# Squared norms of K and Q moved from the attention loop into the QKV stage, and a per-head bound prepared half a head early

## What is computed

```
x = x + layernorm(attn(layernorm(x)))
x = x + layernorm(ffn(layernorm(x)))
attn: qkv = h @ Wqkv.T + b; softmax(q k.T / sqrt(128)) v; @ out_w.T + out_b
ffn:  fake_quant(x) @ fake_quant(kernel) + fake_quant(bias); relu; fake_quant
```

## Time and profile before

| quantity | us |
|---|---|
| timed, median of 2 runs | 7679.78 (7638.61 and 7720.94) |
| the profiled execution, its own time | 7434.41 |
| its span on the slowest core, from the first to the last instruction | 7432.8 |
| spans of the 8 cores | 7412.6 to 7432.8 |

### The profile page before, as it was taken

One profiled execution on the slowest core, in us unless ns is written; L12 is line 12 of the kernel. 1 busy time (PEld: TensorE's weight loads), 2 busy tenths in 40 slices (PEclk: granted clock), 3 DMA queues, 4 the chain that ended last, 5 costly groups with the idle time before them and its releaser, 6 DMA issues.

```text
span 7432.8 us, 43416 instructions; the slowest of 8 cores (7412.6 to 7432.8 us)
## 1 busy us (share of the span) xinstructions
PE 4127.7 (56%) x16028; PEld 1555.4 (21%) x16028; DVE 2157.3 (29%) x2411; ACT 1295.3 (17%) x1457; POOL 93.5 (1%) x106
## 2 busy tenths in 40 slices
PE   0049999987666666667766666664443413030303
PEld 0024444432222222222222222221111101010101
DVE  4512221111111111111111111121221255757566
ACT  1300000003333333333333333320000000000001
POOL 0000000000000000000000000000000000000000
PEclk9999999998888888888888888876666656565656
DMA  6553221111000000000000000029999940000010
GB/s 167 192 127 71 60 68 44 44 49 34 23 23 23 23 23 23 23 23 23 1 23 23 23 23 23 3 50 162 154 157 168 156 80 28 31 31 31 25 40 23
DMA packets 372388, 431.24 MB, mean 58 GB/s; under 512 B 178931, under 2 KB 334579, under 8 KB 355283
## 3 DMA queue, kind: packets, MB, share of 16 engines
q0 software_dynamic: 137344, 159.40, 15.1%
q1 hardware_dynamic: 193638, 168.10, 8.0%
q10 hardware_dynamic: 41200, 100.96, 3.8%
HBM read 461.70 MB, written 100.94 MB: 76 GB/s over the span
## 4 chain that ended last, share of the span: by engine, by line
PE 43%; DVE 20%; ACT 15%; DMA 13%; issue 4%; DVEq 3%; SPq 2%; ACTq 0%; POOLq 0%
PE psB L442 9%; DMA wob<-wo 9%; PE psA L838 8%; PE psA L847 7%; ACT PT L863 6%; PE psB L509 6%; ACT PT L865 6%; PE psA L1093 3%; PE psC L790 2%; PE psA L1360 2%; PE psD L798 2%; SPq L366 1%; SPq L1336 1%; DVE nkt L694 1%; PE psB L1033 1%
## 5 line engine op out<-in xcount | busy, mean ns | idle before, releaser
L442 PE MATMUL psB<-h1fm,wfc 128*128 128x512 bf16 x3072 | 665.8, 380 | 471.4 <-DMA h1fm<-h1h 471.4
L863 ACT ACTIVATE PT<-psA 128x1024 bf16<-128x1024 f32 x512 | 524.4, 1024 | 1596.6 <-PE psA L847 1596.6
L838 PE MATMUL psA<-negCB,onesm 128*128 128x512 bf16 x2048 | 580.2, 409 | 350.8 <-ACT PT L865 279.3
L885 DVE CAST ctxst<-psC 128x512 bf16<-128x512 f32 x64 | 44.3, 691 | 2440.9 <-PE psD L798 2440.9
L1353 PE MATMUL psA<-bqB,onesm 128*128 128x512 bf16 x64 | 27.6, 431 | 1090.7 <-DMA xqfm<-xqh 749.4
L847 PE MATMUL psA<-Qh,Kh 128*128 128x512 bf16 x2048 | 624.5, 435 | 0.0
L790 PE MATMUL psC<-PT,Vh 128*128 128x512 bf16 x2048 | 578.7, 409 | 26.7 <-ACT PT L865 26.7
L798 PE MATMUL psD<-PT,ones_bf 128*1 128x512 bf16 x2048 | 525.0, 378 | 0.0
L865 ACT ACTIVATE PT<-psA 128x1024 bf16<-128x1024 f32 x512 | 521.8, 1019 | 0.0
L442 PEld LDWEIGHTS psB<-h1fm,wfc 128*128 128x128 bf16 x3072 | 301.1, 98 | 835.6 <-issue 474.9
L509 PE MATMUL psB<-wvb,h1fm 128*128 128x512 bf16 x2048 | 468.9, 382 | 0.0
(11 more groups left out here) (175 smaller groups left out, 3156.2 us busy)
## 6 DMA issues: line engine op xcount, KB each, us to landing
wob<-wo POOLq DMA_DIRECT2D x64, 2048.0 KB, 20.7
xst<-x SPq DMA_DIRECT2D x32, 1024.0 KB, 5.3
ktst<-kernT SPq DMA_DIRECT2D x16, 1024.0 KB, 6.7
wfc<-wqk POOLq DMA_DIRECT2D x32, 512.0 KB, 7.8
h1h<-h1t ACTq DMA_DIRECT2D x32, 512.0 KB, 2.8
khh<-kout ACTq DMA_DIRECT2D x16, 1024.0 KB, 8.5
vhh<-vst ACTq DMA_DIRECT2D x128, 128.0 KB, 1.7
Kh<-khh SPq DMA_DIRECT2D x16, 1024.0 KB, 7.1
```

The costliest lines, as they stand in the source:

```text
L442: ins = nc.tensor.matmul(psB[g % 2][:], wfc[fc % 2][:, dc * 128:(dc + 1) * 128], h1fm[:, dc * 4096 + tt * 512: dc * 4096 + (tt + 1) * 512] ...
L838: nc.tensor.matmul(pa[:, off:off + 512], onesm[:], negCB[:], start=True, stop=False, skip_group_check=True)
L863: nc.scalar.activation(PT[sp][:, 0:1024], psA[0][:], AF.Exp, scale=SMS)
```

## The change

1. In stage 2, behind the last group of each Q or K head, the squared norms are now made from `qout` or `kout`, piece by piece of 512 tokens: VectorE squares a piece into `nsq2` (one buffer), TensorE sums it into one of four rows of `psA`, VectorE takes the maximum (K) or copies the row to `nrow2` (Q). Q rows go to DRAM (`nqh`), the 16 maxima of K too (`mkh`).
2. In stage 3 the chain at the head of each head is gone. `emit_cchain` does the rest of it (load of the row, logarithm, halving plus K term, exponential, scaling) for head h+1 behind the second block (`qt == 1`) of head h, and for head 0 at the start of the stage. `negCrow` has two buffers.
3. To make room, `kst` has one buffer instead of two; its load for head h waits until head h-1 is quantised.

```
+        for tt in range(ntt):
+                v.drain()
+                v.tensor_mul(nsq2[:], obuf[par][:, tt * 512:(tt + 1) * 512],
+                             obuf[par][:, tt * 512:(tt + 1) * 512]
+                             ).then_inc(c_sq3.h, 1)
+            wt("tensor", c_sq3, c_sq3.n)
+                nc.tensor.matmul(pa[0:1, off:off + 512], ones_bf[:, 0:1],
+                                 nsq2[:], start=True, stop=True
+                                 ).then_inc(c_nm.h, 1)
+            wt("vector", c_nm, c_nm.n)
+                v.drain()
+                if is_q:
+                    v.tensor_copy(nrow2[0:1, tt * 512:(tt + 1) * 512],
+                                  pa[0:1, off:off + 512]).then_inc(c_nr.h, 1)
+                else:
+                    v.reduce_max(nkt[0:1, tt:tt + 1], pa[0:1, off:off + 512],
+                                 axis=AX).then_inc(c_nr.h, 1)
...
+    def emit_cchain(hh):
+        if hh >= 1:
+            wt("sync", c_negC, hh)
+            nc.sync.dma_start(nq_sb[0:1, :], nqh[hh:hh + 1, :]
+                              ).then_inc(d_nq[hh % 2].h, 16)
+        wt("scalar", d_nq[hh % 2], d_nq[hh % 2].n)
+            nc.scalar.activation(kqa[0:1, :], nq_sb[0:1, :], AF.Ln)
+            v.tensor_scalar(kqt[0:1, :], kqa[0:1, :], 0.5,
+                            lnmk[0:1, hh:hh + 1], OP.mult, OP.add)
+            nc.scalar.activation(kqa[0:1, :], kqt[0:1, :], AF.Exp)
+            nc.vector.tensor_scalar(negCrow[par2][0:1, :], kqa[0:1, :],
+                                    -1.001 / 128.0, -1.0 / 128.0,
+                                    OP.mult, OP.add).then_inc(c_negC.h, 1)
...
-        if h >= 2:
-            wt("sync", f_kn[par], h // 2)
+        if h >= 1:
+            wt("sync", f_kn[0], h)
...
+        wt("tensor", d_k3[par], 16 * (h // 2 + 1))
+        wt("tensor", d_q3[par], 16 * (h // 2 + 1))
...
             emit_pvden(qt, 7)
+            if qt == 1 and h + 1 < H:
+                emit_cchain(h + 1)
```

More of the change, by code:

```diff
@@ L56, in build_program @@
     denh = nc.dram_tensor("denh", [64, 512], F32, kind="Internal").ap()
+    nqh = nc.dram_tensor("nqh", [16, 2048], BF16, kind="Internal").ap()
+    mkh = nc.dram_tensor("mkh", [1, 16], F32, kind="Internal").ap()
     sksh = nc.dram_tensor("sksh", [2048], F32, kind="Internal").ap()
@@ L114, in build_program @@
     c_sq3 = sem("c_sq3")
+    d_nq = [sem("d_nq0"), sem("d_nq1")]
+    s_nq = sem("s_nq")
     c_nm = sem("c_nm")
@@ new lines, in build_program, with _ @@
+        if is_q:
+            @on("vector")
+            def _():
+                v = nc.vector
+                v.drain()
+                v.tensor_scalar_max(nrow2[0:1, :], nrow2[0:1, :], 1e-6
+                                    ).then_inc(c_nr.h, 1)
+            c_nr.inc(1)
+            wt("scalar", c_nr, c_nr.n)
+            if head >= 2:
+                wt("scalar", s_nq, s_nq.n - 16)
+            @on("scalar")
+            def _(head=head):
+                nc.scalar.dma_start(nqh[head:head + 1, :], nrow2[0:1, :]
+                                    ).then_inc(s_nq.h, 16)
+            s_nq.inc(16)
+        else:
+            @on("vector")
+            def _(head=head):
+                v = nc.vector
+                v.drain()
+                v.reduce_max(sm1[0:1, head:head + 1], nkt[0:1, 0:8], axis=AX
+                             ).then_inc(c_nr.h, 1)
+            c_nr.inc(1)
@@ L470, in build_program, with _ @@
+    @on("vector")
+    def _():
+        v = nc.vector
+        v.drain()
+        v.tensor_scalar_max(sm1[0:1, 0:16], sm1[0:1, 0:16], 1e-12
+                            ).then_inc(c_nr.h, 1)
+    c_nr.inc(1)
+    wt("scalar", c_nr, c_nr.n)
+    @on("scalar")
+    def _():
+        nc.scalar.dma_start(mkh[0:1, :], sm1[0:1, 0:16]).then_inc(s_nq.h, 16)
+    s_nq.inc(16)
     wt("tensor", c_bias, 1)
@@ L601, in build_program, with _ @@
         p3be.inc(1)
+    wt("sync", s_nq, s_nq.n)
+    @on("sync")
+    def _():
+        nc.sync.dma_start(nkt[0:1, :], mkh[0:1, :]).then_inc(d_mk.h, 16)
+    d_mk.inc(16)
+    wt("scalar", d_mk, d_mk.n)
+    @on("scalar")
+    def _():
+        nc.scalar.activation(lnmk[0:1, :], nkt[0:1, :], AF.Ln
+                             ).then_inc(p1s.h, 1)
+    p1s.inc(1)
+    wt("vector", p1s, p1s.n)
+    @on("vector")
+    def _():
+        nc.vector.drain()
+        nc.vector.tensor_scalar_mul(lnmk[0:1, :], lnmk[0:1, :], 0.5
+                                    ).then_inc(c_nr.h, 1)
+    c_nr.inc(1)
+    def emit_cchain(hh):
+        par2 = hh % 2
+        if hh >= 1:
+            wt("sync", c_negC, hh)
+        wt("sync", c_nr, 1)
+        @on("sync")
+        def _(hh=hh):
+            nc.sync.dma_start(nq_sb[0:1, :], nqh[hh:hh + 1, :]
+                              ).then_inc(d_nq[hh % 2].h, 16)
+        d_nq[hh % 2].inc(16)
+        wt("scalar", d_nq[hh % 2], d_nq[hh % 2].n)
+        @on("scalar")
+        def _():
+            nc.scalar.activation(kqa[0:1, :], nq_sb[0:1, :], AF.Ln
+                                 ).then_inc(p1s.h, 1)
+        p1s.inc(1)
+        wt("vector", p1s, p1s.n)
+        @on("vector")
+        def _(hh=hh):
+            v = nc.vector
+            v.drain()
+            v.tensor_scalar(kqt[0:1, :], kqa[0:1, :], 0.5,
+                            lnmk[0:1, hh:hh + 1], OP.mult, OP.add
+                            ).then_inc(c_sq3.h, 1)
+        c_sq3.inc(1)
+        wt("scalar", c_sq3, c_sq3.n)
+        @on("scalar")
+        def _():
+            nc.scalar.activation(kqa[0:1, :], kqt[0:1, :], AF.Exp
+                                 ).then_inc(p1s.h, 1)
+        p1s.inc(1)
+        wt("vector", p1s, p1s.n)
+        @on("vector")
+        def _(par2=par2):
+            nc.vector.drain()
+            nc.vector.tensor_scalar(negCrow[par2][0:1, :], kqa[0:1, :],
+                                    -1.001 / 128.0, -1.0 / 128.0,
+                                    OP.mult, OP.add).then_inc(c_negC.h, 1)
+        c_negC.inc(1)
+    emit_cchain(0)
     smm_rel = {}
@@ L644, in build_program @@
[L644 to L743, removed]
@@ L904, in build_program @@
         s_ctx[par].inc(16)
-        wt("vector", d_kn[par], 16 * (h // 2 + 1))
+        wt("vector", d_kn[0], 16 * (h + 1))
         wt("vector", p3be, p3be.n)
@@ L911, in _ @@
             v = nc.vector
-            v.tensor_mul(kqt[:], kst[par][:], RSKb[:])
+            v.tensor_mul(kqt[:], kst[0][:], RSKb[:])
             v.drain()
```

92 lines of the change are left out of this document (39 added, 53 removed).

## The result

The changed kernel takes 7713.73 us at the median of 12 executions (7496.69 to 7851.44), the kernel before 7541.08 us at the median of 10 (7432.84 to 7720.94). The ratio is 1.0105, with a 95% interval of 1.0059 to 1.0151: slower, by about 1%.

The account below looks back on a forecast made before the run. TensorE was taken to bound stage 2, working without a break, with about 1060 us idle in attention. Terms -430 - 22 + 66 + 408 + 68 = +90 gave 7524 us profiled, 7773 timed; 8 in 10 range 7630 to 7870.

Parts of the forecast that it names:

- The first of its cases: Whole kernel: the summed forecast, +93 us on the timed scale, 7773 us, own range 7700 to 7845; chance 0.58.
- the step to the timed scale: Whole kernel: timed median taken as 3.3% above the profiled execution, so +90 became +93 us and 7773 us timed.
- Chain removed between heads: Attention, between heads: first bound matmul of a new head starts 28.7 us earlier, 15 times, -430 us.
- Head 0: Start of attention: L816 starts at 1689.9 instead of 1712.27, -22 us.
- Chain inserted: Attention, behind the second block: the chain delays the third block by 4.4 us, 15 times, +66 us.
- Squares and sums: Stage 2, behind each Q or K head: TensorE waits through steps of 2.16 us each, +408 us.
- The clock after each gap: Stage 2: the first group behind each gap starts at a low clock, 32 losses of 2.1 us, +68 us.
- Attention otherwise: Rest of attention: the head restarts as it did, nothing taken; up to +45 us as the upper bound.
- Stages behind attention: After attention: the sum held no term for these stages.
- The fourth case: Stage 2: excess of timed runs lies in unbroken stretches, gaps give back 137 us; -47, timed 7631; chance 0.13.
- The rival of slow hand-overs: Stage 2's 160 steps: 0.46 us both ways, a step of 2.67, +172 us, timed 7857; chance 0.20.
- That of a clock that stays up: Stage 2's gaps: steps of 1.87 us and no cold start, -24 us, timed 7655; chance 0.09.

Follow-up runs that it names:

- experiment 7: Changed kernel with stage 2's steps in the next head's stream, chain spread over the second block, quantisation behind the next head's first cast: 6894.43 us.
- experiment 4: Changed kernel with the bound's chain taken apart and spread behind the exponentials of steps 2 and 4 of the second block: 7435.41 us.
- experiment 1: Changed kernel without the 192 squares, small sums and maxima of stage 2, their rows filled with a constant: 7032.33 us.
- experiment 3: Changed kernel with each of the 192 steps of stage 2 made twice: 7907.8 us.
- experiment 8: Changed kernel with two buffers for the squares in stage 2, the next square made ahead of the maximum: 7356.76 us, 0.9919 to the kernel before.
- experiment 9: Kernel before with two unread VectorE products of 2.29 us each ahead of the second block's evacuation: span of 7502.8 us on core 1, 81 more than before.
- the fillers: Changed kernel with six large matmuls into an unused accumulator ahead of each small sum of stage 2: 7402.36 us.

## Why the prediction came out as it did

The forecast was slower by 1.2%, and 1.05% was measured. The first of its cases, with the largest chance, took place; what it gave as within 2% is, by the interval, a slow-down of 0.6 to 1.5% and not no change. My sum pointed that way, and only the bound of 2% made it "the same". Two steps failed all the same: the step to the timed scale, and in the sum the term for attention. Term by term, on core 1 or as a mean where it says so:

- *Chain removed between heads:* -28.7 us each; the gap fell from 44.27 to 15.85, -28.4. Right, also in what is late next; experiment 7 removed that, and nothing stood behind it.
- *Head 0:* -22; -25 from the end of V to the first L853.
- *Chain inserted:* +4.4 each; 3.22 to 7.39, that is +4.2 over all 16 heads, since the last has none: 4.45 where it stands. Right, and experiment 4 took it back.
- *Squares and sums:* +408; gaps of 8.36 and 17.08 us less 0.22 each, 16 of each, are 400. A step is 2.06 us and not 2.16, for the most part because a third of the small matmuls (62 of 192) still ran at 2.4 GHz; I had given that to one or two per gap. The experiments 1, 3 and 8 confirm its working.
- *The clock after each gap:* +68; the first group takes 5.40 instead of 3.45, 62 us.
- *Attention otherwise:* "I take nothing". This step failed: -22 us, the largest miss of the sum. I had held that "the head restarts as it did". But the low stretches moved: a block had 6.4 us at 1.2 GHz before, and the four have 8.0, 5.5, 8.3 and 3.8 now. Experiment 9 shows that a longer gap alone moves them. The time at 1.2 GHz is nearly the same in sum (25.8 and 25.6 us a head), and the gain did not come in experiment 9, so where it comes from stays open.
- *Stages behind attention:* nothing; +18 on core 1 and 7 as a mean of four cores, also open.
- The sum was +90 for a profiled execution; measured are +64 between the shortest executions and +73 on core 1.

The step to the timed scale failed as well, and the range stood on it. "The timed median is 3.3% above the profiled execution; scaled by it": the 3.3% came from two executions. Over ten, the median of the kernel before is 1.5% above its shortest, 7432.84 us. The changed kernel's shortest, 7496.69, lies under the 7630 that was my lower end, while the sum before the scaling, 7524, is 27 us from it. That the median of 7713.73 is near 7773 is luck, as its distance from the shortest, 2.9%, is no term of the sum.

What the excess consists of stands in the profile after. The first window is of core 5, the second of core 6 of the same die, both in the V part (columns as above):

```profile
1912.00:2030.00 118.00, 115.58 (x441) 47.64 (x438) 18.31 (x27) 0.00 (x0) 0.53 (x1) 0.81 0.09 29
```

```profile
1880.00:1990.00 110.00, 109.42 (x500) 49.79 (x509) 20.74 (x30) 0.00 (x0) 0.00 (x0) 1.00 0.11 36
```

Core 5 has a granted clock of 0.81, and a matmul in its stream takes 0.27 us instead of 0.22. So there is a third level; the prediction's "no run here shows a third level" was true of the trace before and is not true of this one. The Trainium skill (TensorE: Matmul & The Clock Gate, section "Part 1: The HAM clock gate") states it as a drop of the whole die's clock to 13/16, which is 0.81, once three of its cores run dense matmuls. The trace agrees on the level, and not on when it comes: in the kernel before, eight cores ran 666 us of dense matmuls at 1.00, and here cores 4 and 5 have it while 6 and 7 do not.

The fourth case put the excess into the unbroken stretches of stage 2. They are a place where it occurs, but its conclusion, that gaps would give the excess back, did not come true. From the first to the last large matmul, the Q and K part with its gaps takes 1240 us on core 5 and 1109 on core 1, 131 of the 266 us by which the span of core 5 exceeds that of core 1; 90 are in the V part and 47 in attention. In experiment 9, whose Q and K part has no gaps, it is 769 us on core 4 and 665 on core 1, 104 more. The two timed executions behind the 3.3% have no trace; that their excess is of this kind is inferred.

The rival of slow hand-overs fell: 0.15 us from a square to its small matmul and 0.15 back, in the timeline of the first gap. That of a clock that stays up did not take place, and the fillers showed what the clock would have been worth, 94 us.

## What to carry to other kernels

A small piece of work moved from a stall to a place where the engine was busy cost here as much as the stall had, and far less once it went into the stream of that engine with its operand ready: the same 192 sums cost 460 us between the heads and 94 us among the groups (18 of these for the last head's eight, which stayed in a row). Count for such a move the whole round over both engines, one after the other, and what the clock loses behind it; then ask which order of the lists would take the wait out. A change that gives nothing may hold a good one: its attention half alone was worth 400 us.

## What was not expected of the hardware

- A matmul with one weight column among matmuls with 128 costs 0.42 us in the stream at 2.4 GHz, 0.1 us at each change on top of its own 0.22.
- Six matmuls of unused work in each 1.9 us step kept the granted clock at 1.00 and made the kernel 94 us faster.
- Two cores of a die ran dense matmuls at a granted clock of 0.81, 0.27 us each, while the two others of the same die ran theirs at 1.00 in the same stretch of the program.
- A delay of 4.2 to 4.9 us ahead of one attention block went with a next block that is shorter by 0.9 to 1.4 us and a delayed block that is itself longer by 0.3 to 0.7 (means over the heads), with 3.8 to 4.7 us at 1.2 GHz in the one and 8.3 to 9.4 in the other, where each had 6.5.
